# Expert stage of a two-layer graph network: all first-layer weights loaded in the node stage before it, and ScalarE copies half of the results

## What is computed

```python
logits = jnp.einsum('td,hde->hte', x, hash_proj)   # 4 hashes, 64 experts
cand = jnp.argmax(logits, axis=-1)
top_s, top_i = jax.lax.top_k(scores_t, 2)          # each token keeps 2 of its 4 experts
sel = jnp.take_along_axis(cand_t, top_i, axis=1)
...
buf = jnp.zeros((E, C, d), x.dtype).at[se, posc].add(xr)   # tokens sorted into expert slots
h = jax.nn.gelu(jnp.einsum('ecd,edf->ecf', buf, W1), approximate=False)   # 512 -> 32
y = jnp.einsum('ecf,efd->ecd', h, W2)                                      # 32 -> 512
out = y[se, posc] * keep[:, None].astype(x.dtype)          # mean over the 2 is added to x
```

## Time and profile before

| What | us |
|---|---|
| median of three runs | 2737.44 |
| span of the profiled execution | 2733.6 |
| second node stage | about 1616 to 2150 |
| expert stage | about 2152 to 2505 |
| last stage | about 2505 to 2733 |

### The profile page before, as it was taken

How to read it: one execution, slowest core, us unless ns; L and a number is a source line. 1 busy time by engine, 2 the same in 40 slices (tenths; PEclk the granted TensorE clock), 3 DMA queues, 4 the chain that set the end, 5 groups by cost and what they waited for, 6 DMA issues and landing times. The chain is left out here.

```text
span 2733.6 us, 43338 instructions
## 1 busy us (share of the span) xinstructions
PE 2118.0 (77%) x11528; PEld 1261.1 (46%) x11554; DVE 1837.2 (67%) x5188; ACT 988.2 (36%) x2224; POOL 1794.8 (66%) x2144
## 2 busy tenths in 40 slices
PE   8999999957787738999978969999998377774000
PEld 3444444435565526665644426666665244452000
DVE  4776776645555569999951116777777388886675
ACT  1111111115555515777773425555555122220000
POOL 3555555567777458887737755777777667664776
PEclk9999999978999959999999989999999599997555
DMA  5755555548999746888749976666664599996999
GB/s 198 232 190 178 191 184 182 193 147 271 307 314 312 258 154 193 256 260 262 238 180 324 409 285 211 214 220 215 212 214 138 179 342 371 366 338 242 371 383 360
DMA packets 331876, 689.90 MB, mean 252 GB/s; under 512 B 48217, under 2 KB 55347, under 8 KB 331505
## 3 DMA queue, kind: packets, MB, share of 16 engines
q1 hardware_dynamic: 220088, 404.15, 42.7%
q0 software_dynamic: 76720, 218.39, 24.5%
q10 hardware_dynamic: 34825, 64.59, 6.4%
HBM read 416.71 MB, written 287.44 MB: 258 GB/s over the span
## 5 line engine op out<-in xcount | busy, mean ns | idle before, releaser
L2122 POOL DMA_INDIRECT xg<-n_rows,ids x219 | 219.0, 1000 | 109.6 <-PE psum L154 61.6
L148 PE MATMUL psum<-wl,xT 128*128 128x512 f32 x632 | 288.8, 600 | 0.0
L148 PE MATMUL psum<-wg,yT 128*128 128x512 f32 x632 | 285.5, 595 | 0.0
L148 PE MATMUL psum<-wr,xT 128*128 128x512 f32 x632 | 284.1, 592 | 0.0
L337 ACT ACTIVATE xb<-xa,xsc 128x512 f32<-128x512 f32 x79 | 64.2, 814 | 480.3 <-POOL xsc L397 480.3
L384 POOL TENSOR_TENSOR ve<-mv,epst 128x1 f32<-128x1 f32 x79 | 51.1, 647 | 254.1 <-DVE mv L439 254.1
L1688 POOL DMA_INDIRECT slot_tokens<-sl x158 | 169.1, 1070 | 70.9 <-issue 66.9
L2295 POOL DMA_INDIRECT q<-slot_outputs,qs x158 | 167.8, 1062 | 72.3 <-issue 47.8
L154 PE MATMUL psum<-ident,xg 128*128 128x128 f32 x876 | 136.4, 294 | 92.9 <-DVE gT L2236 73.4
L148 PE MATMUL psum<-wc,x1T 128*128 128x264 f32 x632 | 162.8, 402 | 35.0 <-DVE hb L1231 27.4
L148 PEld LDWEIGHTS psum<-wr,xT 128*128 128x128 f32 x632 | 120.1, 190 | 151.2 <-issue 151.2
(11 more groups left out here) (323 smaller groups left out, 5316.5 us busy)
## 6 DMA issues: line engine op xcount, KB each, us to landing
slot_outputs<-yo ACTq DMA_DIRECT2D x54, 1024.0 KB
x_rows<-x SPq DMA_DIRECT2D x158, 256.0 KB, 3.2
edge_sums<-eo SPq DMA_DIRECT2D x29, 1056.0 KB, 6.5
edge_sums<-go SPq DMA_DIRECT2D x29, 1024.0 KB
xT<-in_xTt SPq DMA_DIRECT2D x79, 256.0 KB
xl_rows<-xl SPq DMA_DIRECT2D x79, 256.0 KB
xr_rows<-xr SPq DMA_DIRECT2D x79, 256.0 KB
residual_rows<-xb SPq DMA_DIRECT2D x79, 256.0 KB, 3.8
```

What stands on the lines that cost most here:

```text
L148: last = nc.tensor.matmul(ps, lhs[:, k, :], rhs[:, k, :], start=(k == 0), stop=(k == DK - 1))
L2122: pool.indirect_dma_start(xg[:, t % 8, :], None, XN3, bass.IndirectOffsetOnAxis(ids[:, t:t + 1], 0), bounds_check=NP - 1, oob_is_err=False ...
```

## The change

First, `w1all` becomes a buffer that exists through the node stage, and SyncE loads it there in eight transfers of 512 KB, one with every fourth tile from tile 16 to tile 44. The load in the expert stage goes, and so do the 12 transfers of `up_weights`: the first three groups get their weights by ScalarE's copies like all others. Their ring `we1` and the gather ring `xg` become buffers of the expert stage; `xg` is cleared there by VectorE, slot by slot, and the first eight gathers wait for their slot.

Second, of the four results of a group ScalarE copies the odd two (`odd_result`), between the store of the group before and the weights; VectorE copies the even two.

```diff
-        xg = sb("xg", [P, 8, D])
-        we1 = sb("we1", [P, WR, 4, DK * MF])
+        w1all = sb("w1all", [P, ME, DK * MF])
...
+                def first_layer(t):
+                    if 16 <= t < 48 and t % 4 == 0:
+                        own = slice(ME // 8 * (t // 4 - 4), ME // 8 * (t // 4 - 3))
+                        sp.dma_start(w1all[:, own, :].rearrange("p e c -> p (e c)"),
+                                     M1[:, own.start * DK * MF:own.stop * DK * MF]).then_inc(e_w1, 16)
+
+                tiles_in_turn(NT, ((0, load), (0, unused_slots), (4, load_x), (9, store), (13, store_n),
+                                   (0, first_layer)))
-                sp.wait_ge(g_rw, 1)
-                for t in range(4 * EARLY):
-                    up_weights(sp, t)
+                sp.wait_ge(e_w1, 8 * 16)
...
-                pool.memset(xg[:], 0.0).then_inc(e_lo, 1)
...
-        w1all = sb("w1all", [P, ME, DK * MF], F32, pt)
+        xg = sb("xg", [P, 8, D], F32, pt)
+        we1 = sb("we1", [P, WR, 4, DK * MF], F32, pt)
...
-                sp.dma_start(w1all[:].rearrange("p e c -> p (e c)"), M1).then_inc(p_all, 16)
...
                 for t in range(LISTED):
+                    if t < 8:
+                        pool.wait_ge(p_clear, t + 1)
...
-                    if g < EARLY:
-                        pe.wait_ge(p_w[g], 16 * len(tiles(g)))
-                    else:
-                        pe.wait_ge(p_cp, tiles(g)[-1] + 1 - 4 * EARLY)
+                    pe.wait_ge(p_cp, tiles(g)[-1] + 1)
...
                         if g >= 1:
-                            pe.wait_ge(p_y, t - 3)
+                            pe.wait_ge(*copied(t - 4))
...
-                    if g == EARLY:
-                        act.wait_ge(p_all, 16)
...
+                def odd_result(t):
+                    g = t // 4
+                    if t % 4 == 1 and g >= 3:
+                        act.wait_ge(p_st[g % 3], 16 * (g // 3))
+                    act.wait_ge(p_dn, t + 1)
+                    act.activation(yo[:, t % 12, :], bank[4 + t % 4], ACT.Copy).then_inc(p_yo, 1)
+
                 def store(g):
-                    act.wait_ge(p_y, tiles(g)[-1] + 1)
+                    act.wait_ge(*copied(tiles(g)[-1]))
+                    act.wait_ge(*copied(tiles(g)[-2]))
...
+                for g in range(3):
+                    weights(g)
                 for g in range(NG + 3):
                     if 1 <= g <= NG:
                         gelu(g - 1)
                     if g >= 3:
                         store(g - 3)
+                    for t in tiles(g - 2)[1::2] if 2 <= g < NG + 2 else ():
+                        odd_result(t)
                     if g + 3 < NG:
                         weights(g + 3)
...
+                for s in range(8):
+                    nc.vector.memset(xg[:, s, :], 0.0).then_inc(p_clear, 1)
                 for g in range(NG + 2):
                     for t in tiles(g) if g < NG else ():
                         copy(t)
-                    for t in tiles(g - 2) if g >= 2 else ():
-                        result(t)
+                    for t in tiles(g - 2)[::2] if g >= 2 else ():
+                        even_result(t)
```

More of the change, by code:

```diff
@@ L1591, in gnn_ffn @@
          e_cd, e_ab, e_ti, e_at, e_rk, e_pk, e_sl, e_oh, e_vm, e_os, e_cu, e_pre, e_jk, e_pl, e_tw, e_p2, e_k1,
-         e_k2, e_w, e_i, e_is, e_sk, e_tot) = (
+         e_k2, e_w, e_i, e_is, e_sk, e_tot, e_w1) = (
             sem("e_" + n) for n in ("co lo 0 y try yT g z r x3 nm sq ve rs n3 tr nT lg lc m8 i8 cd ab ti at rk pk sl oh vm os "
-                                    "cu pre jk pl tw p2 k1 k2 w i is sk tot").split())
+                                    "cu pre jk pl tw p2 k1 k2 w i is sk tot w1").split())
         NG4 = -(-NT // 4)
@@ L1608, in by_group @@
             return step
-        p_w = [nc.alloc_semaphore(name=f"p_w{s}") for s in range(WR)]
         p_v = [nc.alloc_semaphore(name=f"p_v{s}") for s in range(WR)]
         EARLY = 3
[L1614 to L1617, removed]
         def down_weights(eng, t):
@@ L1713, in _ @@
                 pool.memset(idr[:], 0).then_inc(e_lo, 1)
-                pool.memset(xg[:], 0.0).then_inc(e_lo, 1)
                 pool.wait_ge(e_i, 4)
-                pool.wait_ge(e_lo, 4)
+                pool.wait_ge(e_lo, 3)
                 def later_rows(t):
@@ L2091, in gnn_ffn @@
         yo = sb("yo", [P, 12, D], F32, pt)
-        w1all = sb("w1all", [P, ME, DK * MF], F32, pt)
-        phase.extend(p_w + p_v)
+        xg = sb("xg", [P, 8, D], F32, pt)
+        we1 = sb("we1", [P, WR, 4, DK * MF], F32, pt)
+        phase.extend(p_v)
         p_ld, p_st = sems("p_ld", 8), sems("p_st", 3)
-        p_all, p_cp = sem("p_all"), sem("p_cp")
+        p_clear, p_cp = sem("p_clear"), sem("p_cp")
         z_eq, z_bs, z_f, z_ix, z_g, z_0, z_st = (sem("z_" + n) for n in "eq bs f ix g 0 st".split())
-        p_tr, p_T, p_up, p_h, p_dn, p_y = (sem("p_" + n) for n in "tr T up h dn y".split())
+        p_tr, p_T, p_up, p_h, p_dn, p_ye, p_yo = (sem("p_" + n) for n in "tr T up h dn ye yo".split())
         NG = -(-LISTED // 4)
@@ L2102, in tiles, with copied @@
             return range(4 * g, min(4 * g + 4, LISTED))
+        def copied(t):
+            return (p_ye if t % 2 == 0 else p_yo), t // 2 + 1
         with nc.Block() as block:
@@ L2236, in copy, with even_result @@
                     nc.vector.tensor_copy(gT[:, t % 8, :, :].rearrange("p k n -> p (k n)"), bank[t % 2]).then_inc(p_T, 1)
-                def result(t):
+                def even_result(t):
                     g = t // 4
@@ L2242, in result @@
                     dve.wait_ge(p_dn, t + 1)
-                    nc.vector.tensor_copy(yo[:, t % 12, :], bank[4 + t % 4]).then_inc(p_y, 1)
+                    nc.vector.tensor_copy(yo[:, t % 12, :], bank[4 + t % 4]).then_inc(p_ye, 1)
+                for s in range(8):
+                    nc.vector.memset(xg[:, s, :], 0.0).then_inc(p_clear, 1)
                 for g in range(NG + 2):
```

1 line of the change is left out of this document (removed).

## The result

The changed kernel took 2712.86 us, median of four runs (2709.06 to 2719.43); the kernel before 2737.48 (2734.61 to 2740.2). The ratio is 0.9912, with a 95% interval from 0.9896 to 0.9927: 20 to 28 us less. The forecast was 2710.

A forecast was written before the change was run, and what follows sets the result against it. VectorE was taken to pace the expert stage, with the transfers close behind. Gains of 5.6 + 14 + 5 + 2.5 = 27 us off the 2733.6 us span make 2706.6; with 3.8 us more, 2710 us, range 2693 to 2727.

The forecast's parts named there:

- the middle's rate of 380 GB/s or more: Sign in the expert stage's middle: transfers would run at 380 GB/s or more without dips.
- waits for rows and stores in place of `gT`: Sign in the expert stage's middle: TensorE's `gT` wait much smaller, a wait for gathered rows or stores in its place.
- the gathers' pace at the end: Sign at the expert stage's end: a period of 5.2 us per group, with GpSimd hardly waiting.
- The start: Expert stage up to the seventeenth gather: without `w1all` in the way, 5.6 us gained (ends 4 and 7).
- the clears: Expert stage's start: VectorE's eight clears of `xg` take 3.9 us of idle time; cost 0, at most 0.5 us.
- The middle: Expert stage, 2190 to 2440: 90.8 MB at 384 GB/s takes 236 us instead of 250, 14 us gained.
- The tail and the drain: Expert stage's end: 5 us gained over the empty tiles, 2.5 us from half the last result copies going to ScalarE.
- ScalarE: Expert stage: ScalarE's work per group with the odd copies, taken at 5.2 us (4.8 to 6.3).
- The slower rival: Expert stage: ScalarE's in-order queue becomes the bound at up to 6.3 us per group, 2747 us; chance 0.07.
- The node stage: Stage before the expert stage: the eight weight loads cost 0, at most 11 us if all exposed.
- The gathers' pace: Rival, expert stage: transfers never hold GpSimd, gathers every 1.305 us set the pace; 45 us gained, 2692 us; chance 0.12.
- the transfers hold all of the middle at 363 GB/s: Rival, expert stage: the transfers get no faster, the middle term is 0, 13 us gained, 2724 us; chance 0.18.

The follow-up runs named there:

- e4: Changed kernel with second-layer weights loaded for the first six groups only, then reused (results wrong); 2696.06 us, ratio 0.9824 to 0.9873.
- e10: Changed kernel with second-layer loads after the sixth group cut from 32 rows to 16, same instructions (results wrong); 2701.69 us.
- e11: Changed kernel with second-layer loads after the sixth group cut to 16 rows and result buffers for four groups instead of three; 2696.14 us.
- e2: Kernel before the change with only the odd results moved to ScalarE, first-layer weights still loaded in the expert stage; 2722.65 us.
- e3: Changed kernel with result buffers for four groups instead of three; 2711.99 us.
- e5: Changed kernel with ScalarE copying each odd result a second time into a buffer nobody reads; 2721.93 us.
- e6: Changed kernel with each group's store issued right behind its odd copies instead of a turn later; 2719.39 us.
- e7: Changed kernel with result buffers for four groups and each store issued right behind its odd copies; 2714.59 us.
- e8: Changed kernel with VectorE copying all four results and second-layer weights loaded for the first six groups only (results wrong); 2727.23 us.
- e9: Changed kernel with every second-layer weight load issued a second time into a buffer of its own; 2806.32 us.

## Why the prediction came out as it did

**The mechanism held.** The change runs into the transfers in the middle and into the gathers at the end; e4, e10 and e11 show the first, the rows of the last groups the second. The sum was 27 us, the stage gained 21.2 by the profiled executions and the medians differ by 24.6, with an interval of 20 to 28. That the forecast of 2710 came within 3 us of 2712.86 is partly luck: by the stage the sum was 6 us too large, and some 4 us of the profiled difference lie outside the stages that the change touches. The terms' own misses are below. Of the signs that the prediction named, one did not come: the middle's rate of 380 GB/s or more. The others did: waits for rows and stores in place of `gT`, the eight loads with TensorE busy throughout, and the gathers' pace at the end.

**The start** was predicted at 5.6 us and gained 4.9. First use came after 3.4 instead of 5.1 us, which changed nothing, since the seventeenth gather's time is GpSimd's pace; what I left out is the 0.7 us by which the first gather waits for VectorE's first clear (1.44 against 0.74 us into the stage). I had costed the clears at 0 to 0.5.

**The middle is the term that was mis-sized**: 14 us, measured 8.3. The step that failed is taking 384 GB/s, the mean of two undisturbed windows of 28 and 62 us, as what the transfers could hold for 250 us. Over the whole middle the runs at full bytes that wait for transfers hold 366 to 371 GB/s (after, e2, e3, e5, e6, e7), e11 368 with fewer. With 369 instead of 384 the forecast's own sum gives 246 us for its stretch of 250, a gain of 4; another 3.6 lie in the first 11 us of the middle, which that stretch leaves out and where the kernel before moved 251 GB/s (2178.83 to 2190). That makes 7.6 of the 8.3 us measured. It restates the measured rate; that the transfers set it is what e10 and e11 show. By an estimate from the Trainium skill's limit of about 358 GB/s to memory per core (DMA: Bandwidth & Descriptors, Specifications) this term would have been a loss of 4 us; the traces held 3% more than that for 245 us. The same table's 368 GB/s, which it calls the vendor's cost-model derate, lies within the 366 to 371 of the traces. I also left out that the loop before had its own limit near 249 us (e8), so two limits, near 249 and 246, stood behind the 254.5; that the waits where they alternate make up the rest is not shown.

**The tail and the drain** were 5 and 2.5, and measured 1.7 and 6.3: 7.5 against 8.0 together. VectorE's row of result copies is 1.29 us for two instead of 2.48 for four, as expected; what I put on the wrong side of the last gather is the backlog. Seven gathered tiles stood behind it before, four after, and that time is saved after the last gather, not ahead of it. The tail keeps 44.7 us, because its first 10 us still carry the middle's stores; in e4, where they don't, it is 40.4 = 31 x 1.30, GpSimd's pace.

**ScalarE** was taken at 5.2 us a group (4.8 to 6.3) and measured 4.59 near the end. The reason I gave, that the odd copies fill the slow time behind a store, agrees with e6: without them there the round is 5.66. The slower rival did not come true (e5).

**The node stage** at 0: right, 534.5 against 535.1 us. The saved `memset` and the `up_weights` transfers gave nothing that can be told from one execution against another.

**The rivals.** The gathers' pace is reached only with bytes taken away (e4, 226.4 us). That the transfers hold all of the middle at 363 GB/s fell too, but by little: they held 369, between that and the 384 of the forecast and nearer to the rival.

What stays open: why these transfers hold 370 GB/s and not more, and whether a kernel that really needs fewer bytes of second-layer weights could be had; none was tried, and no version that computes the whole result beat the change (the nearest are e7 with 0.9915 and e3 with 0.9917, against 0.9912).

## What to carry to other kernels

A window of 30 to 60 us at a high transfer rate shows what the loop asked for in a good stretch, not what the engines hold; give the rate of the longest full stretch to the slow end of the range and the best short windows to the fast end (here 363 and 384 GB/s, and 369 came). A share near 1.00 does not show by itself that the transfers are the limit: e4 has 1.00 at 356 GB/s with the gathers as the pace, and e9 0.98 at 336 behind SyncE's queue. When one engine is relieved, price every other limit by itself (here VectorE 249, transfers 246, GpSimd 223 us): the gain is the distance to the next, and here the loop with two close limits took longer than either alone, 254.5 us against 249 and 246. An experiment that adds bytes must not add instructions to a queue that is nearly full: change the size of the transfers, not their number.

## What the runs showed of the hardware

SyncE, which reads an expert's number before each weight load, issues one every 1.1 us at the start of the stage in the changed kernel (six within 5.86 us from 2150.34 on) and every 1.5 us near its end (six within 7.86 us from 2445.76 on), without waiting for another engine in either; it needs 7.0 us for four tiles when each load is issued twice. At 15 us less of middle (e11) it had 3.7 us to spare.

ScalarE's weight copies, each with a register read, slow down right behind a 1 MB store: they come every 0.64 us at the start of the stage and every 1.23 to 1.25 us behind the store in e6 (2466.24, 2467.47, 2468.72). That it is the read that takes longer is inferred, since the profile shows only idle time there. Two copies of 128x512 out of PSUM take 1.08 us; with them in that time the round is 4.59 us, against 5.66 with the weights right behind the store.
